# Decoder layer, seam between self-attention and cross-attention: first query gather moved to SyncE, last attention pair split into two steps through one PSUM bank

## Time and profile before

| | us |
|---|---|
| median of 3 runs (1588.66 to 1591.57) | 1589.13 |
| the profiled execution, whole time | 1590.26 |
| its span | 1588.5 |
| TensorE busy in the span | 1521.3 (96%) |
| VectorE busy | 1141.3 (72%) |
| ScalarE busy | 847.6 (53%) |
| mean granted clock, of full speed | 0.972 |

### The profile page before, as it was taken

The page is one execution under the profiler, slowest core; times in us unless marked ns, Lnnn a source line. Parts: engine busy times, 40 slices in busy tenths (PEclk is TensorE's granted clock), DMA queues, the critical chain, the costliest instruction groups (busy, mean ns, idle before and its releaser), DMA issues.

```text
span 1588.5 us, 28790 instructions
## 1 busy us (share of the span) xinstructions
PE 1521.3 (96%) x11272; PEld 1079.8 (68%) x11272; DVE 1141.3 (72%) x2311; ACT 847.6 (53%) x1121; POOL 367.9 (23%) x399
## 2 busy tenths in 40 slices
PE   6999999888799999999999899999999999999998
PEld 3333333334466666666657788898989888888887
DVE  5445556456789999999964788767676777777675
ACT  4888889764588888888873242222222122222221
POOL 0000001221546665666461320000000000000000
PEclk8999999986799999999998999999999999999999
DMA  7765665444467575665652100000000000000000
GB/s 146 136 109 119 127 119 97 83 76 88 62 97 112 77 110 92 103 97 79 97 172 67 32 29 14 1 1 14 1 14 1 14 1 14 1 1 14 1 14 14
DMA packets 61575, 97.24 MB, mean 61 GB/s; under 512 B 12588, under 2 KB 29880, under 8 KB 61440
## 3 DMA queue, kind: packets, MB, share of 16 engines
q1 hardware_dynamic: 60928, 94.62, 32.1%
q10 hardware_dynamic: 512, 0.79, 0.3%
HBM read 26.16 MB, written 4.19 MB: 19 GB/s over the span
## 4 chain that ended last, share of the span: by engine, by line
PE 88%; DVE 7%; ACT 3%; issue 1%; DMA 1%; POOL 0%; POOLq 0%; SPq 0%; ACTq 0%; DVEq 0%
PE ps L109 83%; PE ps L1134 2%; ACT PX L1301 1%; ACT H L538 1%; DVE NM L1356 1%; DVE EE L660 1%; PE ps L1096 1%; PE ps L1142 1%; DVE XC L1961 1%; PE ps L1066 1%; PE ps L1769 0%; DMA QT<-XSb 0%; PE ps L1760 0%; DVE XH L573 0%; DVE X L585 0%
## 5 line engine op out<-in xcount | busy, mean ns | idle before, releaser
L1356 DVE TENSOR_REDUCE NM<-ps 128x4 f32<-128x1024 f32 x256 | 307.9, 1220 | 49.1 <-PE ps L109 47.8
L1301 ACT ACTIVATE PX<-ps 128x1024 f32<-128x1024 f32 x256 | 262.4, 1025 | 82.2 <-PE ps L109 81.0
L538 ACT ACTIVATE H<-ps,b1c 128x1024 f32<-128x1024 f32 x256 | 268.5, 1118 | 38.7 <-PE ps L109 37.1
L1921 ACT ACTIVATE GF<-ps,cols 128x512 f32<-128x512 f32 x128 | 88.2, 689 | 295.7 <-PE ps L109 295.7
L109 PE MATMUL ps<-XC,W_sw_w 128*128 128x512 f32 x768 | 187.3, 395 | 0.0
L109 PEld LDWEIGHTS ps<-XC,W_sw_w 128*128 128x128 f32 x768 | 141.6, 190 | 28.3
L2112 DVE CAST GH<-GF 128x512 fp32r<-128x512 f32 x192 | 82.1, 427 | 106.9 <-ACT GF L1921 101.7
L2220 POOL TENSOR_SCALAR RSc<-AGc 128x4 f32<-128x4 f32 x23 | 6.9, 302 | 602.4 <-DVE AGc L2007 602.4
L109 PE MATMUL ps<-PX,VT 128*32 128x256 f32 x2048 | 140.9, 394 | 1.6 <-DVE X L585 1.5
L1916 ACT ACTIVATE GF<-ps 128x512 f32<-128x512 f32 x64 | 38.2, 597 | 188.5 <-PE ps L109 188.5
L109 PE MATMUL ps<-KT,QT 48*128 48x512 f32 x512 | 133.6, 522 | 5.1 <-DMA QT<-XSb 3.1
(11 more groups left out here) (233 smaller groups left out, 2569.3 us busy)
## 6 DMA issues: line engine op xcount, KB each, us to landing
ST<-QS SPq DMA_DIRECT2D x256, 96.0 KB, 2.8
KT<-KS SPq DMA_DIRECT2D x128, 192.0 KB, 4.7
QT<-XSb SPq DMA_DIRECT2D x120, 96.0 KB, 4.2
XT<-in_xT_dram SPq DMA_DIRECT2D x8, 512.0 KB, 4.3
raw_a<-in_x_dram SPq DMA_DIRECT2D x8, 512.0 KB, 4.4
CR<-in_ctxT_dram SPq DMA_DIRECT2D x8, 512.0 KB, 4.8
out_dram<-X SPq DMA_DIRECT2D x7, 512.0 KB, 3.3
R_sw_w<-in_sw_w_dram SPq DMA_DIRECT2D x6, 512.0 KB, 5.3
```

Of the source, the lines that this page charges most:

```text
L538: e.activation(H1[s % 8][:, :, :], PP[s % 3][:, :, :], ACT.Tanh, bias=b1c[:, half:half + 1], scale=1.0).then_inc(act_th, 1)
L1301: e.activation(PX[s % 3][:, :, :, :], PP[2][:, :, :].rearrange("p g (c q) -> p g c q", c=2), ACT.Exp, bias=0.0, scale=0.25).then_inc(act_e ...
L1356: e.tensor_reduce(NM[u % 2][:, qc, :, :, i], PP[qc][:, :, :].rearrange("p g (m k) -> p g m k", m=2), AX.X, ALU.max, negate=True).then_inc( ...
L1921: e.activation(g[:, :], o, f, bias=cols[:, col:col + 1], scale=1.0).then_inc(act_g, 1)
```

## The change

The eight DMAs of the first queries go from ScalarE's steps -17 to -14 (J = 64) to SyncE's step -33 (J = 60), without the wait for w1; the target QT0 lies over QS1, bd and wor, whose last readers the three other waits cover. The last pair is taken out of `attend_due` and attended one batch at a time, both in bank 7, after the step of phase B on both engines: u = 0 in J = 70 (after step 10), u = 1 in J = 74 (after step 14). The semaphores pe_att and dve_x1 still count to the same ends.

```diff
     def attend_due(J):
-        return due(J, 14, 8, NP)
+        return due(J, 14, 8, NP - 1)
+
+    def last_due(J):
+        return due(J, NJ + 6, 4, 2)

# TensorE, phase A
+        def attend_last(u, free):
+            p, r = NP - 1, 64 + 32 * u
+            w.wait_ge(d_ta, 32 * (p + 1))
+            w.wait_ge(dve_mb, p // 2 + 1)
+            w.wait_ge(*free)
+            for v in range(2):
+                t = mm(e, P[7][:, 256 * v:256 * v + 256], TA[r:r + 32, 128 * v:128 * v + 128], MB[r:r + 32, :], v == 0, True)
+            t.then_inc(pe_att, 1)
+            return dve_x1, 2 * p + u + 1
...
             n = due(J, 6, 4, NIT)
-            if n is not None and (at is None or J >= NJ):
+            if n is not None and at is None:
                 free[7] = norms(n, free[7])
...
-            if n is not None and at is not None and J < NJ:
+            if n is not None and at is not None:
                 free[7] = norms(n, free[7])
             if J >= NJ:
                 for s in soon(J):
                     step(s)
+            u = last_due(J)
+            if u is not None:
+                free[7] = attend_last(u, free[7])

# VectorE, phase A
-        def attended(p):
-            w.wait_ge(pe_att, p + 1)
+        def attended(p, u, b):
+            w.wait_ge(pe_att, p + 1 + (u if p == NP - 1 else 0))
             w.wait_ge(d_xm, 16 * (p + 1))
-            for u in range(2):
-                x1 = X1[:, 4 * p + 2 * u:4 * p + 2 * u + 2, :]
-                e.tensor_tensor(x1, P[6 + u][:, :].rearrange("q (v n) -> q v n", v=2), XM[:, 2 * u:2 * u + 2, :], ALU.add).then_inc(dve_x1, 1)
+            x1 = X1[:, 4 * p + 2 * u:4 * p + 2 * u + 2, :]
+            e.tensor_tensor(x1, P[b][:, :].rearrange("q (v n) -> q v n", v=2), XM[:, 2 * u:2 * u + 2, :], ALU.add).then_inc(dve_x1, 1)
...
             at = attend_due(J)
-            if at is not None and J < NJ:
-                attended(at)
+            if at is not None:
+                for u in range(2):
+                    attended(at, u, 6 + u)
...
             for s in soon(J):
                 step(s)
-            if at is not None and J >= NJ:
-                attended(at)
+            u = last_due(J)
+            if u is not None:
+                attended(NP - 1, u, 7)

# SyncE, phase B
+        def first_queries():
+            w.wait_ge(dve_w, 4)
+            w.wait_ge(pe_g, 1)
+            w.wait_ge(pool_xs, 3)
+            for i in range(4):
+                for g in range(2):
+                    h = 2 * i + g
+                    dma(e, f32(QT[0][64 * g:64 * g + 48, i, :, :]).rearrange("r b t -> r (b t)"), f32(XS[16 * h:16 * h + 16, 0, :, :]), d_ld[0][i])
...
         def step(s):
+            if s == -33:
+                first_queries()

# ScalarE, phase B
-        def first_queries(i):
-
-            after_stack(w, 14)
-            w.wait_ge(dve_w, 4)
-            w.wait_ge(pe_g, 1)
-            w.wait_ge(pool_xs, 3)
-            for g in range(2):
-                h = 2 * i + g
-                dma(e, f32(QT[0][64 * g:64 * g + 48, i, :, :]).rearrange("r b t -> r (b t)"), f32(XS[16 * h:16 * h + 16, 0, :, :]), d_ld[0][i])
-
         def step(s):
-            i = due(s, -17, 1, 4)
-            if i is not None:
-                first_queries(i)
```

## The result

The first comparison gave 1579.86 us (median of 4) against 1589.54: ratio 0.9941, 95% interval 0.9924 to 0.9957. Forecast 1576, range 1570 to 1584. Two later comparisons on other occasions, 12 runs each, gave 1587.14 us, 0.9977 (0.9961 to 0.9993), and 1584.36 us, 0.9973 (0.9955 to 0.9991). The changed kernel is faster, in the later comparisons by some 4 us (3.7 and 4.3 by the ratios) and not by the 13.3 that I summed; its single runs lie between 1576 and 1592 us. One run of the kernel before (1833.24 us) and one of g3 (1670.55 us) had a far lower clock than their neighbours throughout and are left out of every comparison.

What follows compares the result with a forecast made beforehand. TensorE was taken as the bound, with time to gain only where it idles or runs at half clock in the seam; 8.5 + 4.8 = 13.3 us off 1590.26 gives 1577.0, as a median 1576, range 1570 to 1584.

Steps and rivals of the forecast that it cites:

- The sum of 13.3 us: Whole kernel: 8.5 us from moving the queries plus 4.8 us from attending the last pair by batch.
- Part 1, the issue on SyncE: SyncE's gap before the keys: eight query issues take 5.1 to 7.7 us, keys go out at most 2.2 us later.
- the cover: First seam: the first keys land by about 341 us, TensorE needs them at 345.17, leaving 4 us.
- The 4.1 us that the queries might have stood in front of the keys: SyncE's queue: if drained in order, the eight queries' 0.79 MB delay the keys' landing by at most 4.1 us.
- Part 1, the sure term: First seam: TensorE's wait for the queries between the last w2 and the first maxima goes, 3.1 us.
- Part 1, the term for the clock: First seam: without the hole the clock stays near 1.00 from 345 to 360 us, bringing the queries' gain to 8.5 us.
- the first rival: First seam: the clock falls again soon after 345 us, the queries' move gains only 3.1 to 4 us; 1580.8 us, chance 0.19.
- Part 2, step 10 in front of the attend: Second seam: from turn_o to maxima(25) 3.7 to 4.2 us instead of 9.9, gaining 5.7 to 6.2 us.
- Part 2, the price of the second batch: J = 74: half an attend (0.5 us) and half the add give back 0.6 to 1.7 us, taken as 1.2.
- The one in which part 2 is given back: J = 74 to 77: the second attend waits behind late VectorE, losing the gain of J = 70; 1580.6 us, chance 0.13.
- the clock rival: Same as the first rival: the clock falls again after 345 us; 1580.8 us, chance 0.19.
- The stall of 2.07 us before 430.48: TensorE's 2.07 us stall hangs on the norm of pair 7 in J = 77 and stays.

Runs made afterwards that it cites:

- g3: e3's kernel with one extra 128x128 filler matmul behind each maxima of steps -14 to -1: 1580.84 us, 0.9949 of the kernel before.
- e4: Changed kernel with the eight query DMAs at step -33 issued by ScalarE instead of SyncE: 1589.80 us, 1.0003 of the kernel before.
- e1: Kernel before with only the first queries moved to SyncE's step -33, last pair attended as before: 1587.18 us, 0.9983 of the kernel before.
- e3: Changed kernel, but the last pair attended by the old eight-record attend in banks 6 and 7, after step 10: 1580.25 us, 0.9945 of the kernel before.
- g2: Changed kernel with the last pair's second batch attended in J = 72 instead of J = 74: 1583.01 us, 0.9962 of the kernel before.
- g4: e3's kernel with GpSimd's norm root behind the steps of phase B for periods from 64 on: 1577.83 us, 0.9930 of the kernel before.
- f3: e3's kernel measured again in another group: 1581.74 us, 0.9954 of the kernel before.
- e2: Changed kernel with the queries moved back to ScalarE, last pair still one batch at a time in bank 7: 1588.97 us, 0.9999 of the kernel before.
- e0: Changed kernel measured again, unaltered, against the kernel before: 1587.14 us, 0.9977.

## Why the prediction held, and where it was wrong

- **The number.** The first comparison's 1579.86 us lies in the range, and that was in part luck: its four runs lie between 1577.0 and 1582.5, while 17 of the 24 later runs of the same kernel lie above 1584, and so do both later medians, 1584.4 and 1587.1. (That the first comparison's chip played a part is possible; no run tells.) The sum of 13.3 us stands against 9.7 us between the medians in the first comparison, and 3.7 and 4.3 us by the ratios in the later ones.
- **The bound.** TensorE's two stops in the seam, and their sizes, were read rightly, and both changes shortened the stage that they aimed at (w2 to t0, 23 to 26). What the other stages then did with it is where the sum failed.
- **Part 1, the issue on SyncE: right.** Eight issues in 6.09 us (forecast 5.1 to 7.7), the keys 1.4 us later (at most 2.2), no wait for them: the cover was there. The 4.1 us that the queries might have stood in front of the keys did not appear: the last query landed at 335.2, and the first two keys landed 3.70 and 4.35 us after their issue, against 3.79 and 4.53 before. The Trainium skill (DMA: Bandwidth & Descriptors, Queues, rings and completion order) says that each DMA engine goes round between its queue rows and works through one row in ring order; the trace cannot decide on it, since the queries had all landed 1.7 us before the first key did. e4 shows what the same issues cost where there is no cover.
- **Part 1, the sure term: right.** 3.1 us forecast, 3.2 in the traces, 2.7 as a whole kernel (e1, interval 1.1 to 4.3).
- **Part 1, the term for the clock: wrong.** The step that failed is the full clock behind the missing hole ("PEclk near 1.00 from 345 to 360"), on which 5.4 of the 8.5 us stand. No run shows these 5.4 us. Without filler the clock fell 5.7 to 8.1 us after the start of the last w2 in every trace with part 1, and 4.5 us after it in the kernel before: taking the hole away did not keep the clock up, and the first rival was right in that. The anchors at GpSimd and SyncE moved by 3.1 us instead of 5.8; and 8.5 was not even between its own two ends, 5.8 + 3 = 8.8 and 11. From the last w2 to reduction 23 the profiled runs gained 5.7, 3.7 and 6.0 us in the changed kernel, 5.6, 6.0, 6.1 and 5.6 in e3, e4, g2 and g4, 2.1 in e1 and f3, and 2.8 in e2, which has no part 1. So what comes on top of the hole, from 1.1 us less to 2.9 us more, goes by how long the clock was low in the stage 12 to 23, as the table's last column shows.
- **Part 2, step 10 in front of the attend: right.** 4.4 us for 9.9 (forecast 3.7 to 4.2, so just above it); and e3 beside e1 shows that this place is the gain.
- **Part 2, the price of the second batch: wrong.** Half of attend, put at 1.03 us at the low clock and half of that at full, was 1.10 us at full clock for each half. I had taken the duration of eight records as divisible; in the old order the two batches' matmuls alternate and run in pairs that start within 35 ns, and the split leaves each without its partner. And the 0.6 to 1.7 us put on what is given back in J = 74 left out the clock: in five of six traces it falls behind that attend, and reductions 26 to 92 then take 127.5 to 128.5 us instead of 123.0 (first changed trace). That is 4.5 to 5.5 us, nearly all that part 2 had gained; alone no worth of it is shown (e2, 0.9999, 0.9988 to 1.0009).
- **The rivals.** The one in which part 2 is given back had 0.13 and 1580.6 us; with the clock rival's 0.19 beside it, the two together describe the typical run. The prediction named no spread between executions, and it should have: it had noticed that the clock falls at waits, and not drawn from this that the same program could run with and without the fall. What makes the spread is only in part known. e2 and e4 have the same second attend, their traces fell there too, and their twelve runs each lie within 5.0 and 5.7 us, where the changed kernel's lie within 14.5 and 14.4.
- **The stall of 2.07 us before 430.48** hung on the norm's root in front of OC, as the text said of the norm of pair 7; g4 shows it.

Open: what makes the clock fall at one wait of a microsecond and not at another; g2 and the changed kernel differ in it with like waits (g2 waits 1.56 us before 407.03 without a fall). Which stages differ from trace to trace is read from one trace of each kernel (three of the changed one), so the stage table shows where time can go, not how often. That e4 and e0, or f3 and g4, ran in different groups leaves some uncertainty in their difference, though each has its own kernel before. The faster versions g4 and e3 were not combined with other places of the batch.

## What to carry to other kernels

What is taken out of one critical wait can be lost at the next ones: here 4 to 6 us gained at J = 70 went again in the half clock behind two waits of 0.4 and 1.0 us. Where matmuls of 32 rows alternate over two banks, splitting them in time can double their price: ask of a duration of many records whether its parts overlap. Moving DMA issues cost nothing in a gap of SyncE, and 3.5 us where ScalarE's instruction stream was full. Compare many executions: the same program differed by 14.5 us on one chip, and four runs gave 0.9941 where twelve gave 0.9977.

## What was not expected of the hardware

- The clock fell to its lower level with TensorE 74% busy and no wait over 0.54 us since the last w2 (changed kernel, 348 to 352 us: 2.95 of 4 us busy, clock 0.71 on average), and it stayed at 1.00 where TensorE was 61% busy (g2, 404 to 408 us).
- A filler of one 128x128 matmul a step was enough to hold it to 366 us, where it falls at 349 without (e3).
- Four attend records take 1.10 us and eight 1.13 us, both at full clock: the records of the two batches start within 35 ns of each other.
- The changed kernel's runs lie between 1576.2 and 1591.7 us, those of g4 between 1575.3 and 1581.5.

The stretch in which the clock fell:

```profile
348.00:352.00 4.00, 2.95 (x14) 1.77 (x13) 4.00 (x5) 0.38 (x1) 0.61 (x1) 0.71 0.10 14
```
